# A transformer block on one core: routing weights of groups two to seven come from DRAM by repeating loads instead of turns and 0-1 products

## The reference, cut to what matters

```python
scores = softmax((x @ wt.T + repeat(g @ wg.T, s)) / 2)        # E = 8 experts
topk_w, topk_idx = top_k(scores, 2); topk_w = topk_w / (topk_w.sum(-1) + 1e-20)
gp = leaky(einsum('th,ehm->etm', x, w_gate))                  # M = 64 rows for each expert
up = einsum('th,ehm->etm', x, w_up)
y_all = einsum('etm,emh->eth', gp * up, w_down)
y = sum over the token's two experts of topk_w * y_all        # plus a shared expert of 128 rows
```

## Time and profile before

| | us |
|---|---|
| median of 3 runs (824.22 to 825.05) | 824.92 |
| the profiled execution's own time | 822.76 |
| its span, first to last instruction | 821.0 |
| PE busy | 786.9 |
| ACT busy | 606.6 |
| DVE busy | 584.7 |
| POOL busy | 448.9 |

### The profile page before, as it was taken

One profiled execution on the slowest core, in us unless ns is written; L12 is line 12 of the kernel. 1 busy time (PEld: TensorE's weight loads), 2 busy tenths in 40 slices (PEclk: granted clock), 3 DMA queues, 4 the chain that ended last, 5 costly groups with the idle time before them and its releaser, 6 DMA issues.

```text
span 821.0 us, 16705 instructions
## 1 busy us (share of the span) xinstructions
PE 786.9 (96%) x5368; PEld 595.9 (73%) x5368; DVE 584.7 (71%) x1581; ACT 606.6 (74%) x1652; POOL 448.9 (55%) x388
## 2 busy tenths in 40 slices
PE   5979989999999999999999999999999999999997
PEld 4756766677866877677777777768776777777786
DVE  5768897867678676976678677776678886665632
ACT  2335786699758978589767987589775989789974
POOL 3128966943666454953559355763549564854300
PEclk9999999999999999999999999999999999999999
DMA  7050001000010001000010000000010000000000
GB/s 254 1 193 2 24 33 30 2 1 2 1 44 1 1 1 43 1 1 2 2 43 1 2 1 24 21 1 1 1 44 1 2 1 2 2 14 1 14 1 14
DMA packets 15589, 16.99 MB, mean 21 GB/s; under 512 B 1408, under 2 KB 13072, under 8 KB 15120
## 3 DMA queue, kind: packets, MB, share of 16 engines
q1 hardware_dynamic: 15200, 15.91, 6.0%
q10 hardware_dynamic: 304, 0.01, 0.0%
HBM read 13.81 MB, written 2.11 MB: 19 GB/s over the span
## 4 chain that ended last, share of the span: by engine, by line
PE 54%; ACT 19%; DVE 8%; issue 7%; POOL 5%; DVEq 0%; ACTq 0%; POOLq 0%
PE ps_M L1202 25%; ACT sb_sm L733 8%; PE ps_S L1321 5%; PE ps_z L1349 4%; PE ps_T L1336 4%; PE ps_T L1329 4%; PE ps_M L1248 4%; ACT L733 3%; PE ps_M L1381 3%; DVE sb_sm L1089 2%; ACT sb_al L774 2%; ACT L774 2%; PE ps_S L1303 2%; POOL sb_rq L617 2%; ACT sb_pT L740 2%
## 5 line engine op out<-in xcount | busy, mean ns | idle before, releaser
L733 ACT ACTIVATE sb_sm<-sb_sm,sb_nmx 128x129 f32<-128x129 f32 x512 | 199.2, 392 | 33.3 <-DVE sb_nmx L1097 32.8
L634 POOL TENSOR_TENSOR sb_sm<-sb_sm,sb_rden 128x512 f32<-128x512 f32 x128 | 135.8, 1064 | 144.9 <-DVE sb_rden L1102 144.9
L627 POOL TENSOR_TENSOR sb_biasm<-sb_bias,sb_maskn 128x512 f32<-128x512 f32 x128 | 170.9, 1343 | 79.0 <-DVE sb_sm L1089 55.0
L1089 DVE SCALAR_TENSOR_TENSOR sb_sm<-ps_S,sb_rq,sb_biasm 128x129 f32<-128x129 f32 x512 | 140.5, 342 | 55.9 <-PE ps_T L1329 43.2
L617 POOL TENSOR_TENSOR sb_rq<-sb_qss,sb_mhalf 128x16 f32<-128x16 f32 x32 | 92.1, 2903 | 27.4 <-DVE sb_qss L1074 27.4
L1321 PEld LDWEIGHTS ps_S<-sb_k,sb_qs 64*128 64x128 f32 x1024 | 65.1, 187 | 43.6 <-issue 43.1
L733 ACT ACTIVATION_READ_ACCUMULATOR sb_sm<-sb_sm,sb_nmx 128x1 f32 x512 | 96.6, 189 | 0.0
L740 ACT ACTIVATE sb_pT<-ps_T 128x512 f32<-128x512 f32 x128 | 74.4, 588 | 22.3 <-PE ps_T L1329 22.2
L1321 PE MATMUL ps_S<-sb_k,sb_qs 64*128 64x129 f32 x1024 | 83.0, 291 | 4.4 <-DVE sb_sm L1089 3.5
L1097 DVE TENSOR_REDUCE sb_nmx<-sb_sm 128x4 f32<-128x516 f32 x128 | 85.5, 675 | 0.4
L1329 PE MATMUL ps_T<-sb_ident,sb_sm 128*128 128x128 f32 x512 | 76.5, 276 | 3.6 <-POOL sb_sm L634 3.2
(11 more groups left out here) (256 smaller groups left out, 1733.9 us busy)
## 6 DMA issues: line engine op xcount, KB each, us to landing
sb_xg<-in_xT SPq DMA_DIRECT2D x8, 256.0 KB, 4.1
sb_xs<-in_x SPq DMA_DIRECT2D x8, 256.0 KB, 4.6
sb_qs<-in_xT SPq DMA_DIRECT2D x1, 2048.0 KB, 10.0
sb_hA<-in_h SPq DMA_DIRECT2D x2, 1024.0 KB, 6.7
out_y<-sb_res SPq DMA_DIRECT2D x7, 256.0 KB, 2.3
sb_sm<-toeplitz SPq DMA_DIRECT2D x1, 1024.0 KB, 5.8
sb_rows<-in_rows SPq DMA_DIRECT2D x1, 648.0 KB, 6.3
sb_oT<-in_wq SPq DMA_DIRECT2D x1, 512.0 KB, 10.4
```

The lines of the kernel that those rows point to most:

```text
L627: pool.tensor_tensor(biasm[:, heads, 1:NK], bias0[:, heads], maskn[:, j // 4].unsqueeze(1).broadcast_to([128, 4, S]), ALU.add)\
L634: pool.tensor_tensor(sm[:, heads, 1:NK], sm[:, heads, 1:NK], rden[:, heads].unsqueeze(2).broadcast_to([128, 4, S]), ALU.mult)\
L733: ins = act.activation(sm[:, h], sm[:, h], ACT.Exp, bias=nmx[:, h:h + 1], accum_out=den[:, h:h + 1])
L1089: ins = dve.scalar_tensor_tensor(sm[:, h], bank(g, "sim", n, odd)[:, m * NK:(m + 1) * NK], rq[:, k * HEADS + h:k * HEADS + h + 1], biasm[: ...
```

## The change

For groups 2 to 7 the third expert tile is no longer made by PE. In the fill, PE turns the finished weights of all 32 sequences once (`wr`: two 128 x 128 transposes), ACT copies them to SBUF, SP stores them to a DRAM tensor `routes` (256 rows of 128 tokens). For each of the groups 2 to 7, SP then loads from it eight times (`wb`): each load fills 64 partitions of one quarter of `hA` with one expert's four rows, repeated (partition step 0 in the source). DVE's L958 multiplies by `hA[:, c]`, in SBUF, instead of by the PSUM tile. Groups 0 and 1 keep `rw` and the 0-1 products, as their loads could not be ready.

`hA` is free for this between `l4` of one group and `l3` of the next, so `load_weights` of group g waits for `l4` of group g - 3, and `gelu3` of group g waits until the experts of group g + 2 have been multiplied. `n3` becomes a tensor of its own, `route2` keeps 8 sequences, `ones` moves into `n3`. The steps `rw` of PE, ACT and DVE are gone from "steady" and "seventh", SP's queue in "steady" is `rw.0 maskn.0 wb.0 l4.0`, and the orders of all engines are written anew in nearly all iterations.

```diff
+USES = {"wr": "M", "rw": "M", "exp": "MMM", ...
-    rings = "MM" if (step, k) == ("exp", NX - 1) else USES.get(step, "")
+    rings = "MM" if step == "exp" and (k == NX - 1 or g > 1) else USES.get(step, "")
...
-        n3, zT = hA[:, 0].rearrange("p (b d) -> p b d", b=GB), [t[:, 0] for t in hBs]
+        n3, zT = sb("n3", [128, GB, D]), [t[:, 0] for t in hBs]
...
             def load_square(g, k):
-                sp.wait_ge(*((routed, 2 * ROUTE_OPS), (parts_low["h1"], 1))[k])
+                sp.wait_ge(*((routes_psum.sem, 1), (parts_low["h1"], 1))[k])
+            def store_routes(g, k):
+                sp.wait_ge(routes_copied.sem, routes_copied.at(g, 1))
+                sp.dma_start(routes.rearrange("(n p) s -> p n s", p=128), routes_T...).then_inc(routes_stored, 16)
+            def load_weights(g, k):
+                if g == 2:
+                    sp.wait_ge(routes_stored, 16)
+                    sp.wait_ge(parts_low["h2"], 1)
+                else:
+                    sp.wait_ge(l4_psum.sem, l4_psum.at(g - 3, 1))
+                for half in range(2):
+                    for c in range(NC_):
+                        src = bass.AP(tensor=routes.tensor, offset=(g * GB * E + 2 * c + half) * S,
+                                      ap=[[0, EM], [E * S, GB], [1, S]])
+                        sp.dma_start(hA[half * EM:(half + 1) * EM, c]..., src).then_inc(w_loaded.sem, 16)
...
             def gelu3(g, o):
+                if g + 2 < NG:
+                    act.wait_ge(hidden.sem, hidden.at(g + 2, NC_))
...
             def expert(g, c):                       # DVE
-                    dve.wait_ge(expert_psum.sem, expert_psum.at(g, 3 * c + 3))
+                    if g < 2:
+                        dve.wait_ge(spread_psum.sem, spread_psum.at(g, c + 1))
+                        weight = bank(g, "exp", c, 2)[:]
+                    else:
+                        dve.wait_ge(w_loaded.sem, w_loaded.at(g - 2, 128))
+                        weight = hA[:, c]
-                    dve.tensor_tensor(hT[:, c], bank(g, "exp", c, 2)[:], gs[:, c % 2], ALU.mult)
+                    dve.tensor_tensor(hT[:, c], weight, gs[:, c % 2], ALU.mult)
...
             def ln_z(g, k):
-                dve.wait_ge(l4_psum.sem, l4_psum.at(min(g, NG - 1), 0))
...
             def expert(g, c):                       # PE
-                if c < NC_:
+                if c < NC_ and g < 2:
+            def routes_turn(g, k):
+                pe.wait_ge(routed, 2 * ROUTE_OPS)
+                for n in range(2):
+                    pe.transpose(ps[:, n * S:(n + 1) * S], route[:, n * S:(n + 1) * S], ident[:])
```

Two of the orders, "steady" of PE and DVE, as far as `PT.3` and `l1.3`:

```diff
 "pe steady"
-        rw.0 sim.0 exp.0-1 sim.1 exp.2-3 sim.2 exp.4 down.0 PT.0 zT.0 sim.3 qkv.0 PT.1 l1.0-2 PT.2-3 l1.3 ...
-        ... kv.0 q.0-2 sim.10 PV.4-5 sim.11 z.3 l4.0 q.3 PT.12 q.4 PT.13 z.4 q.5 PV.6 qs.0-3 ... z.6-7
+        sim.0 exp.0-1 sim.1 exp.2-3 sim.2 exp.4 down.0 PT.0 zT.0 sim.3 PT.1 qkv.0 l1.0-1 PT.2-3 l1.2-3 ...
+        ... q.0 sim.10 PV.4-5 sim.11 z.3 q.1-3 PT.12 l4.0 q.4 z.4 q.5 PT.13 qs.0-3 PV.6 ... z.6-7
 "dve steady"
-        rw.0 xl.0 ln3.0 sim.0 exp.0-1 sim.1 exp.2 max.0 exp.3 max.1 inv.0 sim.2 max.2 inv.1 max.3 exp.4 zT.0 ...
+        xl.0 ln3.0 sim.0 exp.0-1 sim.1 exp.2 max.0 exp.3 max.1 inv.0 max.2 exp.4 zT.0 inv.1 sim.2 max.3 ...
```

More of the change, by code:

```diff
@@ L58 @@
+        warm.15-16 xnT.0 warm.17-18 fl.3 q.0-2 kv.0 q.3-4 qs.0-3 q.5-7 qs.4-7 warm.19 qst.0 kT.0 warm.20-21
     """,
     "pe start": """
[L60 to L63, removed]
+        sim.0 rw.0 exp.0 sim.1 exp.1 sim.2 exp.2-3 sim.3 PT.0-1 exp.4 PV.0 PT.2 sim.4 down.0 PT.3 sim.5 PT.4
@@ L70 @@
+        q.4 z.4 q.5 PT.13 qs.0-3 PV.6 q.6 PT.14 kT.0 z.5 q.7 PT.15 qs.4-7 PV.7 qst.0 z.6-7
     """,
     "pe seventh": """
[L72 to L75, removed]
+        exp.0 sim.0 exp.1-2 sim.1 exp.3 sim.2 exp.4 down.0 zT.0 PT.0 sim.3 PT.1 qkv.0 l1.0-1 PT.2 l1.2-3 sim.4
@@ L120 @@
+        q.4-5 kT.0 ssq.0 vs.0 ssc.0 q.6-7
     """,
     "dve start": """
-        xl.0 rw.0 sim.0 max.0 sim.1 exp.0 max.1 exp.1 sim.2 inv.0 max.2 inv.1 exp.2 max.3 inv.2 exp.3 sim.3
-        inv.3 max.4 sim.4 inv.4 max.5 exp.4 max.6 inv.5 down.0 sim.5 inv.6 max.7 pl.4 qkv.0 scores.0 sim.6 inv.7
-        max.8 mix.0 sim.7 inv.8 max.9 ln1.0 sim.8 inv.9 max.10-11 ln2.0 inv.10 sim.9 xnT.0 max.12 inv.11 sim.10
-        inv.12 max.13-14 q.0 kv.0 sim.11 q.1 maskn.0 inv.13 q.2-3 max.15 q.4 inv.14 kT.0 inv.15 q.5 pl.5 ssq.0
@@ L126 @@
-        q.6 ssc.0 q.7 vs.0
+        xl.0 rw.0 sim.0 max.0 exp.0 sim.1 inv.0 max.1 exp.1 sim.2 inv.1 exp.2 max.2 exp.3 inv.2 max.3 sim.3
+        max.4 inv.3 exp.4 sim.4 max.5 inv.4 pl.4 down.0 max.6 inv.5 sim.5 max.7 qkv.0 scores.0 inv.6 sim.6 inv.7
+        max.8 mix.0 sim.7 inv.8 max.9 ln1.0 max.10 inv.9 sim.8 max.11 ln2.0 inv.10 sim.9 inv.11 max.12 xnT.0
+        sim.10 inv.12 maskn.0 max.13 kv.0 q.0 max.14 sim.11 inv.13 max.15 inv.14 q.1-2 pl.5 q.3-4 inv.15 kT.0
+        q.5-6 ssq.0 ssc.0 vs.0 q.7
@@ L134 @@
+        down.0 zl.0 sim.3 inv.3 max.4 qkv.0 l1.0-1 h1.0-1 l1.2-3 sim.4 max.5 h1.2 inv.4 h1.3 inv.5 sim.5 max.6
+        scores.0 inv.6 max.7 h2.0-1 inv.7 sim.6 max.8 mix.0 h2.2-3 sim.7 max.9-10 sim.8 inv.8 max.11 inv.9 ln1.0
+        inv.10 ln2.0 inv.11 sim.9 xnT.0 max.12 kv.0 sim.10 max.13 sim.11 q.0 inv.12 q.1 inv.13 max.14-15 maskn.0
+        q.2-3 inv.14 kT.0 l4.0 q.4 inv.15 q.5-6 ssq.0 q.7 ssc.0 vs.0
     """,
     "dve seventh": """
-        rw.0 xl.0 ln3.0 exp.0 sim.0 exp.1-2 sim.1 max.0 exp.3-4 inv.0 max.1-2 zT.0 inv.1 sim.2 max.3 down.0
@@ L137 @@
-        inv.2 zl.0 inv.3 sim.3 qkv.0 l1.0-1 h1.0 max.4 l1.2 h1.1 sim.4 h1.2 max.5 l1.3 max.6 scores.0 h1.3 inv.4
-        sim.5 inv.5 max.7 inv.6 sim.6 inv.7 max.8 mix.0 sim.7 inv.8 max.9-10 ln1.0 sim.8 max.11 inv.9 h2.0 ln2.0
-        inv.10-11 sim.9 h2.1 xnT.0 h2.2 max.12 h2.3 sim.10 max.13 kv.0 inv.12 max.14 q.0 kT.0 q.1 sim.11 inv.13
-        max.15 maskn.0 inv.14 q.2-5 inv.15 ssq.0 q.6 ssc.0 q.7 vs.0
+        xl.0 ln3.0 exp.0 sim.0 exp.1 max.0 sim.1 exp.2-3 inv.0 max.1-2 exp.4 zT.0 inv.1 sim.2 max.3 down.0 inv.2
@@ L147 @@
+        max.8-9 sim.8 h2.3 inv.8 max.10 inv.9 max.11 ln3d.0 inv.10 zTd.0 sim.9 inv.11 max.12 sim.10 max.13
+        inv.12 max.14 inv.13 zld.0 sim.11 max.15 inv.14 l4.0 l1d.0-1 h1d.0-1 l1d.2 h1d.2 l1d.3 h1d.3 inv.15
+        h2d.0-3
     """,
```

162 lines of the change are left out of this document (92 added, 70 removed).

## The result

| | before | after |
|---|---|---|
| median of 4 and 4 runs beside each other, us | 824.57 (823.84 to 825.05) | 813.24 (812.93 to 815.51) |
| ratio, 95% interval | 1 | 0.9871 (0.9851 to 0.9891) |
| profiled execution, us | 822.76 | 813.36 |
| its span, us | 821.0 | 811.5 |

The page of the kernel after: busy time, the chain's shares by engine, granted clock, and the DMA issues of weights and x (count, KB each, median us to landing). They answer to the earlier trace rows.

A forecast was written before the change was run, and what follows sets the result against it. PE was taken as the bound, DVE and ACT close behind. Six rounds of 1.79 - 0.33 give 8.8 us, less 1.1 once: 7.7 us less, 815.1 profiled, 817.3 for the median; range 810.5 to 823.5.

The forecast's parts named there:

- PE sets the time: Whole kernel: PE, busy 96% of the span, is the bound; DVE is close behind in the experts' stretch, ACT mid-round.
- Removed from PE, 1.79 us a round: Experts' stretch: turns 0.44, four 0-1 products 1.11 and a bank wait 0.24 us go in each of six rounds.
- Can DVE and ACT follow?: Experts' stretch onward: with chunk 4 ahead of `sim.2` in DVE's order, both follow PE's full 1.79 us.
- The lock, 0.33 of a round: L958, now reading SBUF twice, collides with POOL in chunk 3: 0.33 us lost a round, bounds 0 and 1.3.
- second rival: DVE becomes the experts' bound and the lock costs 1.28 us a round: 2.0 us less, 823; chance 0.20.
- shelter: Experts' stretch: chunks 0 to 2 run beside POOL's inverse roots, until 246.23, and lose nothing to the lock.
- The loads: SP's queue: eight issues take 4.0 us, weights land 6 us early, x has 2.5 us of room; steady cost nothing.
- third rival: Loads of 11.6 us make x 2.7 us late in six rounds, 16.2 us: 832; slower from about 10.5; chance 0.10.
- Once, at the end of the start, 1.1 us: Group 2's weight loads delay its x to 141.1, `xh` wanting it near 140: 1.1 us once, bounds 0 and 3.
- Fill, last and drain, 0 with bounds of 2.5: Outside the rounds: the rewritten orders were taken to cost 0, with bounds of -2.5 and +2.5 us.
- The seventh: The seventh round was counted among the six rounds that each gain 1.79 - 0.33 us.
- the whole cut and more: First rival: freed banks and engine holes give 2.3 us in each of six rounds, 13.8 in all: 811; chance 0.15.

The follow-up runs named there:

- e2: After, but chunks 0 to 3 of groups 2 to 7 again reserve a third M bank, left unused: 823.49 us, ratio 1.0008 to before.
- e3: e2 with PE also issuing the four 0-1 products of groups 2 to 7 into the third bank, unread: 825.82 us, ratio 1.0024 to before.
- e11: After, with only POOL's fourth `bias` moved back behind the inverse roots in the steady order: 817.67 us, ratio 0.9921 to before.
- e4: Loads, banks and tensors as after, every engine's order as before, fitted to the changed steps: 830.0 us, ratio 1.0068 to before.
- e9: e4 with POOL's fourth `bias` moved ahead of the inverse roots in the steady order: 826.27 us, ratio 1.0026 to before.
- e10: e9 with chunk 4 and `zT` moved ahead of `sim.2` in DVE's steady order: 829.23 us, ratio 1.0066 to before.
- e7: After, with the eight weight loads of 128 KB split into sixteen of 64 KB: 849.21 us, ratio 1.0293 to before.
- e8: After, with x of the next group loaded a round earlier, ahead of the eight weight loads: 813.18 us, ratio 0.9871 to before.
- e6: After, with only the fill in the order of before on all engines: 811.94 us, ratio 0.9844 to before.

## Why the prediction was right, and where it was not

**PE sets the time.** Right in its outcome: the rounds shorten, and PE's busy time falls by as much as the span does. As the mechanism it is only half right: e2 has less for PE to do as well and gains nothing, since at the borders of the chunks DVE's drain holds PE.

**Removed from PE, 1.79 us a round.** The step whose terms failed. Forecast 1.11 for the 0-1 products, 0.24 for the banks, 0.44 for the turns. Measured 0.29 for the products (e3 against e2) and 1.35 for the banks (e2 against after). For the turns and the new orders together nothing is left: e3, which has the products and the banks but not the turns, has rounds of 94.84, before a mean of 94.79. The table of e3 shows why: the turns' 0.44 us are gone again at the up of chunk 1. So "the chain's pieces" were the wrong measure of what a removed product gives, and one late start of 0.47 us the wrong measure of the banks. With three banks taken PE is held in chunks 1 and 3, and the 0-1 products covered a part of it. That the sum came out near was luck, as my errors nearly cancelled: 1.64 is measured for those two, 1.79 was forecast for all three.

**The lock, 0.33 of a round.** Measured zero in after (24 of 24 at 692 ns). The place was right: chunk 3 against `bias`. The price where it strikes is 1.06 us on DVE and 0.85 on a round (e11). The new POOL order, which I had not followed, keeps the `bias` away. That is the second rival's mechanism, real and not met. The trace of e11 shows a queue, the later operation being late by 1.06 us where the other still had 1.20. Here the Trainium skill ("SBUF — State Buffer", section "SBUF: two separate sides"), by which the second of the two blocks until the first ends, is nearly borne out. I had put 5.7 us less gain at stake by it; e11 loses 4.4 (4.1 by the ratios), hit in five of six rounds. Beside POOL's inverse roots the same rule does not hold as it stands: they read SBUF too and take 2.9 us each, from 235.70 to 247.42 in the round of after shown above, and yet chunk 2's multiplication, in the midst of them, keeps its time.

```profile
245.45 0.69 DVE L999 TENSOR_TENSOR sb_hT<-sb_hA,sb_gs 128x512 f32<-128x512 f32 x1
```

So the "shelter" that I had read from the rows was right.

**Can DVE and ACT follow?** Right in after: net 1.58 a round against the forecast 1.79 - 0.33 = 1.46. It was seen only with the new orders: with the old ones PE waits inside `down` for chunk 4, 1.8 us in e4 and 0.7 in e9, where the lock is away; with chunk 4 moved up alone (e10) DVE waits 1.5 us for ACT. I had used one line of that, chunk 4 ahead of `sim.2`, and taken it as sufficient by itself; e10 shows that it is not.

**The loads.** No wait in steady rounds: right. The sizes were not: eight issues take 5.2 us, not 4.0, landing 3.6 us against my 4.4 to 5.8, and the room of x is 1.2 us instead of 2.5. Of the third rival's two figures neither is confirmed: loads of 11.5 us (e7) do make the kernel slower, but no run tries its threshold of 10.5, and its price was too low, 16.2 us for six times 2.7 us, where e7 has x late by 28.7 us in all and loses 36.6 in these six rounds.

**Once, at the end of the start, 1.1 us.** SP issued the eight at 132.90 (forecast 132.5) and x behind them:

```profile
132.90 5.29 SPq L542 DMA_DIRECT2D sb_hA<-routes  x8
138.23 0.60 SPq L549 DMA_DIRECT2D sb_xg<-in_xT  x1
```

By the median landing it came near 142.3, and `xh`, which started at 142.54, shows no wait for it; the start grew by 0.38 us. With x out of the way (e8) the start is 0.05 us shorter and the round behind it 0.01, so this term was mis-sized: it cost nothing. I had `xh` at about 140; the longer fill alone makes it 2 us later.

**Fill, last and drain, 0 with bounds of 2.5.** +2.07 and -1.06, inside. 1.6 of the fill's 2.07 go with its order (e6). One thing that this order moves is ACT's first `xh`, which starts 7 us later in after, behind `wh`, `rx` and two `pb`; that it is the cause is not shown.

```profile
13.36 0.62 ACT L718 ACTIVATE sb_xh<-sb_xg 128x512 fp32r<-128x512 f32 x1
```

**The seventh.** I gave it a steady round's 1.46; it gave 3.00. With e2's 86.11, 2.18 of this is the banks; with e3's 86.64, 0.53 is the products; the remaining 0.29 has no run of its own.

**The sum.** In the span, forecast 7.7 less, measured 9.5: six rounds 10.9 (8.8 forecast), less 2.07 and 0.38, plus 1.06. The other 2.3 us of the miss are the step from profiled execution to median: I added the 2.16 us of before, and after's median lies 0.12 below its profiled execution. The rival *the whole cut and more* forecast 811 and named freed banks as its cause; that mechanism is the one the runs show, so it deserved more than 0.15.

Not tried: the products with the banks freed, and the number of banks apart from how the ring is dealt.

## What to carry to other kernels

A chain of waits through a busy engine shows what it did, not what it would have saved: before pricing a removed product by its piece of the chain, ask what the engine would wait for at that place, and look at how many buffers a step takes of its ring. A step that takes the whole ring ties the producer to its consumer at every border; giving back one of three was here worth over four times what the products cost while all three were taken. And where all orders are written by hand, a new data path and its orders are one change: each half alone made this kernel slower, here in part by what it did to fill, start and one transfer.
